# First attention of a conv-attention hybrid: TensorE's order of score, transpose and value groups, and ScalarE's order of exponentials and evictions

## The reference

```python
h = layernorm(x, n1_w, n1_b)
win, pad_hw = window_partition(h, WS)            # windows of 14 x 14, image padded to 28 x 28
q, k, v = ...                                    # 12 heads of 16 channels
attn = jnp.einsum('bqc,bkc->bqk', q * scale, k)
attn = (attn.reshape(-1, WS, WS, WS, WS) + rel_h[:, :, :, :, None] + rel_w[:, :, :, None, :]).reshape(-1, N, N)
attn = jax.nn.softmax(attn, axis=-1)
out = jnp.einsum('bqk,bkc->bqc', attn, v)
x = shortcut + (out.reshape(bw, WS, WS, DIM) @ proj_w + proj_b)
```

## Time and profile before

| what | value |
|---|---|
| median of 3 runs | 922.12 us (921.82 to 924.09) |
| the profiled execution | 930.86 us, of which the span of the trace is 929.2 us |
| mean granted TensorE clock | 0.979 of full speed |
| busy over the span | PE 93%, weight loads 75%, VectorE 49%, ScalarE 49%, GpSimd 19% |

### The profile page before, as it was taken

The page is one execution under the profiler, slowest core; times in us unless marked ns, Lnnn a source line. Parts: engine busy times, 40 slices in busy tenths (PEclk is TensorE's granted clock), DMA queues, the critical chain, the costliest instruction groups (busy, mean ns, idle before and its releaser), DMA issues.

```text
span 929.2 us, 14911 instructions
## 1 busy us (share of the span) xinstructions
PE 864.3 (93%) x5408; PEld 693.0 (75%) x5408; DVE 459.4 (49%) x1025; ACT 459.9 (49%) x937; POOL 180.3 (19%) x257
## 2 busy tenths in 40 slices
PE   2899989989989899999998899999999899998998
PEld 1766866866766678878887579975989579984998
DVE  4878778688678633455553630164103640154001
ACT  5887677677677343244443443453233433443232
POOL 3040040040100122245200430035000340025000
PEclk9999989999999799999998999999999999999999
DMA  7010010000000000001003000000000000000000
GB/s 199 1 39 3 0 36 2 0 23 11 0 1 1 26 15 19 12 24 46 13 1 119 0 1 1 1 18 0 0 0 17 0 0 0 0 17 1 1 1 18
DMA packets 12712, 15.50 MB, mean 17 GB/s; under 512 B 5313, under 2 KB 10561, under 8 KB 12545
## 3 DMA queue, kind: packets, MB, share of 16 engines
q1 hardware_dynamic: 10656, 9.46, 3.3%
q0 software_dynamic: 2016, 5.51, 2.1%
HBM read 13.39 MB, written 1.57 MB: 16 GB/s over the span
## 4 chain that ended last, share of the span: by engine, by line
PE 77%; DVE 11%; ACT 5%; issue 5%; DMA 1%; SPq 0%; POOL 0%; DVEq 0%; ACTq 0%; POOLq 0%
PE ps L221 20%; PE ps L1548 13%; PE ps L1475 6%; PE ps L1203 6%; PE ps L1563 5%; PE ps L1121 4%; PE ps L1295 4%; PE ps L1101 3%; DVE area L275 2%; PE ps L1109 2%; PE ps L1333 1%; PE ps L1081 1%; DVE dstat L771 1%; ACT area L911 1%; PE ps L1161 1%
## 5 line engine op out<-in xcount | busy, mean ns | idle before, releaser
L221 PE MATMUL ps<-xs,ws 128*128 128x512 f32 x460 | 128.8, 426 | 5.5 <-DVE xs L502 3.7
L1548 PE MATMUL ps<-area 128*128 128x192 f32 x768 | 127.4, 326 | 0.0
L1548 PEld LDWEIGHTS ps<-area 128*128 128x128 f32 x768 | 124.8, 190 | 2.0 <-issue 0.5
L221 PE MATMUL ps<-ws,wx 128*128 128x512 f32 x480 | 116.2, 397 | 1.3 <-DVE ws L792 1.3
L1049 ACT ACTIVATE area<-ps,bcol 128x512 f32<-128x512 f32 x96 | 65.7, 689 | 86.6 <-PE ps L221 86.6
L221 PEld LDWEIGHTS ps<-xs,ws 128*128 128x128 f32 x460 | 88.7, 202 | 24.9 <-issue 6.6
L221 PEld LDWEIGHTS ps<-ws,wx 128*128 128x128 f32 x480 | 89.2, 188 | 22.8 <-DVE ws L792 3.0
L803 DVE TENSOR_TENSOR area<-ps,area 128x384 f32<-128x384 f32 x32 | 17.9, 559 | 177.8 <-PE ps L1548 177.8
L911 ACT ACTIVATE area<-ps,nm 112x196 f32<-112x196 f32 (+1 forms) x240 | 85.7, 441 | 18.8 <-DVE nm L637 18.8
L414 POOL TENSOR_TENSOR area<-area,dstat 128x512 f32<-128x512 f32 x32 | 33.0, 1042 | 276.6 <-DVE dstat L768 276.6
L637 DVE TENSOR_REDUCE nm<-ps 112x4 f32<-112x784 f32 (+1 forms) x72 | 62.9, 874 | 31.4 <-PE ps L1101 26.4
(11 more groups left out here) (179 smaller groups left out, 1403.5 us busy)
## 6 DMA issues: line engine op xcount, KB each, us to landing
stage<-in_wall POOLq DMA_DIRECT2D x42, 128.0 KB, 2.4
area<-in_w2e SPq DMA_DIRECT2D x1, 2304.0 KB, 8.3
out<-xres SPq DMA_DIRECT2D x4, 384.0 KB, 2.6
xres<-in_x SPq DMA_DIRECT2D x1, 1152.0 KB, 7.8
area<-in_wall SPq DMA_DIRECT2D x2, 512.0 KB, 5.6
area<-in_w2a SPq DMA_DIRECT2D x1, 576.0 KB, 3.7
room<-in_rel SPq DMA_DIRECT2D x4, 128.0 KB, 5.3
xres<-in_x SPq DMA_DIRECT2D x1, 384.0 KB, 3.1
```

The lines of the kernel that those rows point to most:

```text
L221: last = mm(out_, l, r, start=n == 0, stop=n == len(pairs) - 1)
L1548: last = mm(ps[:, 4 + b, s * D:s * D + D], hTd[:, m, b * T + s * P:b * T + s * P + P], w2x[:, e * MC + m, :], start=m == 0, stop=m == MC - 1)
```

## The change

TensorE's loop now takes two rounds at once. For even u the order is S(u), S(u+1), T(u-2), both halves of V((u-4)//2), T(u-1), and behind it F in rounds 4, 8 and 12. ScalarE takes X(u) before E(u-2) in every round. The query projections keep their places among these groups, the first key projection goes behind V(8). No matmul, instruction of VectorE or transfer is added or removed. Every buffer and bank keeps its use, so the waits are the same ones at new places.

```diff
@@ ScalarE, body_a
                 for u in range(UNITS + 2):
-                    if u >= 2:
-                        v = u - 2
...
-                        act.wait_ge(a_t, base + v + 1)
-                        if v >= 4:
-                            act.wait_ge(a_o, it * OUTS + v // 2 - 1)
-                        A.activation(pts[v % 4][0:half, :, 0:wide], ps[0:half, 4:6, 0:wide], ACT.Copy)\
-                            .then_inc(a_pta, 1)
                     if u < UNITS:
...
                         last.then_inc(a_p, 1)
+                    if u >= 2:
+                        v = u - 2
...
+                        A.activation(pts[v % 4][0:half, :, 0:wide], ps[0:half, 4:6, 0:wide], ACT.Copy)\
+                            .then_inc(a_pta, 1)
@@ TensorE, body_a
-                for u in range(UNITS + 4):
+                def scored(u):
+                    rows, parts, keys, i, h = unit(u)
+                    if u >= 2:
+                        pe.wait_ge(a_p, base + u - 1)
+                    gated(pe, 0)
+                    (scores_full(u, i, h) if u < MAIN else scores_border(u, h)).then_inc(a_s, 1)
+
+                def turned(v):
+                    rows, parts, keys, i, h = unit(v)
+                    half = keys // 2
+                    pe.wait_ge(a_p, base + v + 1)
+                    pe.wait_ge(a_pta, 1 + base + v)
+                    for k in range(2):
+                        for n in range(UH * parts):
+                            last = tr(ps[0:half, 4 + k, n * rows:n * rows + rows],
+                                      pp[0:rows, v % 3, n, k * half:k * half + half], ident[0:rows, 0:rows])
+                    last.then_inc(a_t, 1)
...
+                for u in range(0, UNITS + 4, 2):
...
+                    if u < UNITS:
+                        scored(u)
+                        scored(u + 1)
+                    if 2 <= u < UNITS + 2:
+                        turned(u - 2)
+                    if nxt and u >= UNITS:
...
+                        queries(u - UNITS)
+                    if u >= 4:
+                        d = (u - 4) // 2
...
+                        pe.wait_ge(a_pta, 1 + base + 2 * d + 2)
+                        if d >= 2:
+                            pe.wait_ge(a_on, it * OUTS + d)
...
+                        values(d, 0)
+                        values(d, 1).then_inc(a_o, 1)
+                    if 2 <= u < UNITS + 2:
+                        turned(u - 1)
+                    if nxt and u == UNITS:
+                        queries(1)
+                    if nxt and u == UNITS + 2:
+                        pe.wait_ge(a_p, base + UNITS)
+                        keys_of(0)
...
+                    if u in ((4, 8, 12) if nxt else (4, 8)):
+                        if u > 4:
+                            pe.wait_ge(a_on, 1 + it * OUTS + u // 2 - 2)
                         front_turn_part(it + 1, u // 4 - 1, (ln_xt_e, it + 1))
```

More of the change, by code:

```diff
@@ L892, in body_a @@
                 for u in range(UNITS + 2):
-                    if u >= 2:
-                        v = u - 2
-                        rows, parts, keys, i, h = unit(v)
-                        half, wide = keys // 2, UH * parts * rows
-                        act.wait_ge(a_t, base + v + 1)
-                        if v >= 4:
-                            act.wait_ge(a_o, it * OUTS + v // 2 - 1)
-                        A.activation(pts[v % 4][0:half, :, 0:wide], ps[0:half, 4:6, 0:wide], ACT.Copy)\
-                            .then_inc(a_pta, 1)
                     if u < UNITS:
@@ L914, in body_a @@
                         last.then_inc(a_p, 1)
+                    if u >= 2:
+                        v = u - 2
+                        rows, parts, keys, i, h = unit(v)
+                        half, wide = keys // 2, UH * parts * rows
+                        act.wait_ge(a_t, base + v + 1)
+                        if v >= 4:
+                            act.wait_ge(a_o, it * OUTS + v // 2 - 1)
+                        A.activation(pts[v % 4][0:half, :, 0:wide], ps[0:half, 4:6, 0:wide], ACT.Copy)\
+                            .then_inc(a_pta, 1)
                     if u in ((5, 9, 13) if nxt else (5, 9)):
@@ L1177, in body_a @@
                 base = it * UNITS
-                for u in range(UNITS + 4):
-                    if u < UNITS:
[L1180 to L1193, removed]
-                    if 2 <= u < UNITS + 2:
[L1195 to L1206, removed]
@@ new lines, in body_a @@
+                pe.wait_ge(a_qa, it * 4 + 4)
+                pe.wait_ge(a_qw, it * 4 + 4)
+                for u in range(0, UNITS + 4, 2):
+                    if u == MAIN:
+                        pe.wait_ge(a_kae, it * 2 + 2)
+                        pe.wait_ge(a_qb, it * 2 + 2)
+                    if u < UNITS:
+                        scored(u)
+                        scored(u + 1)
+                    if 2 <= u < UNITS + 2:
+                        turned(u - 2)
+                    if nxt and u >= UNITS:
@@ L1210, in body_a @@
                         queries(u - UNITS)
+                    if u >= 4:
+                        d = (u - 4) // 2
+                        if d == 0:
+                            pe.wait_ge(a_ve, it * 6 + 6)
+                        pe.wait_ge(a_pta, 1 + base + 2 * d + 2)
+                        if d >= 2:
+                            pe.wait_ge(a_on, it * OUTS + d)
+                        if d in (1, 3):
+                            pe.wait_ge(ln_xt, 2 * it + 3 + d // 2)
+                        if nxt and d == 5:
+                            pe.wait_ge(ln_xt_e, it + 2)
+                        gated(pe, 0)
+                        values(d, 0)
[4 more added lines that the diff above has]
+                        queries(1)
                     if nxt and u == UNITS + 2:
```

## The result

The changed kernel takes 940.4 us (936.6 to 943.2, 4 runs), the kernel before 923.1 (921.8 to 928.3, 4 runs): a ratio of 1.0173, 95% interval 1.0132 to 1.0215. The forecast was 938. The profiled execution took 942.3, span 940.6, against 930.9 and 929.2 before: 11.5 us more there, where the medians differ by 17.3. The four runs of the changed kernel differ by 6.6 us, and the mean granted clock goes along: 0.980 and 0.980 for 936.6 and 938.5, 0.975 and 0.970 for 942.3 and 943.2.

A forecast was written before the change was run, and what follows sets the result against it. TensorE was taken to bound the settled part, the VectorE and ScalarE chain the first units. Three pairs of images at +4.2 us and 3.4 for the fourth gave +16 on 922.1, so 938 us, range 920 to 946.

The forecast's parts named there:

- The settled round: Middle rounds, S(u) to S(u+2): 5.20 us instead of 5.32, T(u-1) waiting for E(u-2) behind X(u); bounds 4.97 and 5.30.
- The rounds of S(12) and S(14): Two rounds late in each pair of images: 0 gained at S(12), between -0.3 and +0.3; 0.5 of 4.4 us at S(14).
- The last units: End of each pair of images: T(16) waits for E(15) behind X(17), a loss of 1.7 us, 1.2 in the last pair.
- The first units: Start of each pair of images: T(0) stands behind S(3), so S(6) comes 3.0 to 3.9 us later; bounds 1.6 and 5.2.
- the clock will not be back: Within the first units: TensorE stays at the low clock until S(4) and S(5) are done, 3.9 us later instead of 1.6.
- The sum: All four pairs of images: +4.2 us for each of the first three and 3.4 for the fourth, together +16.
- clock back: Rival, first units: the clock returns as before, costing 1.6 us each, a pair of images +2.0, so 930 us; 20%.
- longer cold: Rival: low clock lasts one or two stretches more per pair and follows the wait at T(16), 943 to 949 us; 12%.
- Switches: Rival, faster: only the saved changes between kinds of TensorE groups count, settled round near 4.97, hence 917 us; 14%.
- Cancel: Rival for the whole kernel: gains and losses meet within 0.3%, 919.4 to 924.9 us; 7%.

The follow-up runs named there:

- e2_both_old: The changed kernel with the first rounds as in e1_first_old, and ScalarE taking E ahead of X again for u of 16 and more: 927.3 us, ratio 1.0028.
- pair of filler runs: The changed kernel and the kernel before, each with unused transposes of the identity in TensorE's first waits: 929.9 us and 922.3 us.
- e3_pe_only: The changed kernel with TensorE's new order but ScalarE's old one, E ahead of X in every round: 975.8 us, ratio 1.0536.
- e1_first_old: The changed kernel with the first rounds as before: S(2), T(0), S(3), T(1), and E(0), E(1) ahead of X(2), X(3): 935.2 us, ratio 1.0101.

## Why the prediction was right, step by step

- **The settled round.** Forecast 5.20, measured 5.18, by the chain that was named. S(6) to S(12) took 16.0 to 16.1 where it was 16.7 to 16.8: 0.67 gained, 0.6 forecast. Two joint halves of V take 156.26 - 154.60 = 1.66, the value that had been taken between its bounds. The Trainium skill ("TensorEngine Tiling (Array Packing)", PSUM Bottleneck) says that tiling speeds up TensorE but not the emptying of PSUM. The trace agrees as far as it goes: M, X and E, which all read PSUM, make up about 3.1 of the chain's 5.18 us, and TensorE waits 0.2 us for E; no run changed the tiling itself. The joined groups save what was forecast (1.52 for two S where two starts were 1.70 apart, 1.66 for two halves of V where they were 1.82), but only 0.14 of the 0.34 shows in the round. Whether what they save is the drain at a change of tiling mode that the same page of the Trainium skill names (Key Properties), no run separates.
- **The rounds of S(12) and S(14).** Forecast 0 and 0.5, measured 0.1 and 0.4 to 0.5 in the first three pairs, -0.1 and 0.2 in the fourth.
- **The last units.** Forecast from S(16) to T(16) 5.5, measured 5.5 in three pairs; in the fourth 4.9, a loss of 1.1 where 1.2 had been forecast. E(15) behind X(17) is the cause: e2_both_old puts it back and T(16) comes 4.1 us after S(16). What follows T(16) gave 0.4 back in the first two pairs, 0.2 forecast.
- **The first units: the order right, the clock mis-sized.** The order part was worked out as 1.6 with the clock back as early as before. The pair of filler runs, with no low clock on either side, gives 1.4, and the three pairs whose low clock lasted as long as before give 2.3, 1.0 and 1.7. On top of it the forecast had the low clock until behind T(1) and through S(4) and S(5), in every pair, and put 2.3 us there in the second and third. In the profiled run only the third pair did this, and longer (three stretches of 3.4 us more): S(6) came 2.3, 1.0, 5.0 and 1.7 later, on the mean 2.5, where 3.0 to 3.9 stood in the sum. The term that was mis-sized is thus "the clock will not be back": in three of four pairs it was back 9.7 to 10.6 us after S(0), ahead of T(1), though T(0) was gone from the wait. What decides between the two was not tried.
- **The sum.** 16 forecast, 12.2 in the first attention of the profiled run, 11.5 in its total, 17.3 in the medians. The profiled sum is made of three pairs at 2.5, 1.1 and 1.9, which is what the rival "clock back" said (2.0 each), and one at 6.7, which is what "longer cold" had for a pair (4.2 and one or two stretches at 1.3). That the median agrees with the forecast to 2 us is luck in good part. The profiled run of before was 8 us above its median and had five low stretches in its four pairs (besides the one at the end), that of after only 2 us above its own. The kernel before varies with its clock: in the later series its runs took 921 to 922 us where the mean granted clock was 0.994 to 0.996, and 928 to 932 where it was 0.979 to 0.986. So its median very likely holds less low clock than the profiled run on which the sum was built; which stretches the unprofiled runs had is not recorded.
- **The rivals.** "Clock back" came true in three pairs of four, "longer cold" in one, at the first units and once more behind the wait of T(16). "Switches" fell with the settled round of 5.18, where it needed 4.97, and with e3_pe_only: the saved changes are real, but TensorE cannot use them without ScalarE's new order, and not in the first units. "Cancel" is out: the interval of the ratio starts at 1.0132.

One step in my own account was wrong and shown so: I took the first round as the seat of the first loss. e1_first_old moved the wait to S(5) instead of taking it away; the loss sits in every joint pair of scores whose second member waits for a maximum that VectorE delays, that is in two rounds.

## What to carry to other kernels

Joining two groups of one kind on TensorE saves the gap between kinds, but puts all that stands behind the second of them behind its wait; join them only where both inputs are there, and keep the old order at the start of a pipeline and at its end. Before an engine's work is reordered, look at what the other engines have queued between its inputs: here the statistics and the scaling for a later stage stood ahead of the maxima. A wait on TensorE can cost twice, by its length and by the lower clock behind it, and useless transposes in the wait gave the second part back.

## What the runs showed of the hardware

Sixteen transposes of the identity in a wait of up to 2.7 us kept TensorE at 2.4 GHz through the first attention's four pairs of the kernel before, and 0.6 to 1.9 us per pair came back, 0.5% of the run by its ratio. In the four kernels with filler the clock never fell at the first units, in 16 pairs of images; in the nine without it, it fell in 25 of 36. With the low clock the same T took 1.73 instead of 0.97, joint V 3.25 instead of 1.74.

The same wait did not always bring the low clock. TensorE sat idle for 2.70 us ahead of S(2) in the third pair of e1_first_old as in the kernel before, and there the clock stayed up until the wait of S(5). How long it stays low varied too: 3.4, 6.8 and 13.7 us at the first units of the first, second and third pair of the changed kernel, for the same code in one run. What separates these cases was not tried.
